# A recommender tower on one core: layers 2 and 3 turned round, the last two tables looked up whole, weights loaded later

## The reference

```
e = stack([tbl_0[ids[:, 0]], ..., tbl_25[ids[:, 25]]], axis=1)          # 512 x 26 x 128
all_emb = concatenate([bottom[:, None, :], e], axis=1)                  # 512 x 27 x 128
z = einsum('bfd,bgd->bfg', all_emb, all_emb)[:, TRIU_I, TRIU_J]         # 351 pairs
h = concatenate([z, bottom], axis=1)                                    # 479
h = maximum(h @ W_top1 + b_top1, 0)                                     # 512
h = maximum(h @ W_top2 + b_top2, 0)                                     # 256
y = h @ W_top3                                                          # 512 x 1
```

## Time and profile before

| | us |
|---|---|
| median of 3 runs | 107.83 (107.79 to 108.54) |
| the profiled execution, its own time | 108.94 |
| its span, first to last instruction | 107.2 |
| PE busy in the span | 99.5 (93%) |
| DVE, ACT, POOL busy | 65.0, 55.8, 59.8 |
| mean granted TensorE clock | 1.00 of 2.4 GHz |

### The profile page before, as it was taken

The page is one execution under the profiler, slowest core; times in us unless marked ns, Lnnn a source line. Parts: engine busy times, 40 slices in busy tenths (PEclk is TensorE's granted clock), DMA queues, the critical chain, the costliest instruction groups (busy, mean ns, idle before and its releaser), DMA issues.

```text
span 107.2 us, 3613 instructions
## 1 busy us (share of the span) xinstructions
PE 99.5 (93%) x1546; PEld 84.7 (79%) x1546; DVE 65.0 (61%) x146; ACT 55.8 (52%) x96; POOL 59.8 (56%) x65
## 2 busy tenths in 40 slices
PE   4999699999999999999878999979999989999992
PEld 4766476888888888888767999769898979997970
DVE  5597799999999999999970019005600740092000
ACT  5531959926976994993704324322462427224331
POOL 2777777777877777788777777777730000000000
DMA  2799898748768648995122121221210000000000
GB/s 47 221 337 329 271 282 295 230 68 320 215 135 317 165 137 229 299 269 132 49 55 55 49 55 49 69 64 51 55 54 2 6 6 0 6 6 0 0 0 3
DMA packets 7460, 13.22 MB, mean 123 GB/s; under 512 B 1990, under 2 KB 3881, under 8 KB 7444
## 3 DMA queue, kind: packets, MB, share of 16 engines
q1 hardware_dynamic: 5484, 9.25, 28.1%
q0 software_dynamic: 1792, 3.67, 13.1%
q10 hardware_dynamic: 168, 0.07, 0.3%
HBM read 12.97 MB, written 0.01 MB: 121 GB/s over the span
## 4 chain that ended last, share of the span: by engine, by line
PE 44%; DVE 36%; issue 8%; DMA 6%; ACT 2%; SPq 1%; ACTq 0%
DVE onehot L522 25%; PE acc L709 11%; PE acc L675 11%; DVE lo L505 10%; PE ring L719 7%; DMA raw<-tbl 6%; PE acc L640 6%; PE acc L700 4%; PE ring L652 3%; PE ring L729 2%; PE ring L683 1%; ACT hi L363 1%; DVE raw L493 1%; DVE idt L486 0%; ACT h L467 0%
## 5 line engine op out<-in xcount | busy, mean ns | idle before, releaser
L346 POOL DMA_INDIRECT rows<-tbl,ids_sb x56 | 59.0, 1054 | 18.3 <-issue 16.8
L522 DVE TENSOR_SCALAR onehot<-far 128x512 fp32r<-128x512 f32 x83 | 31.6, 437 | 1.3 <-ACT far L377 1.3
L613 PE MATMUL acc<-onehot,hi 128*128 128x512 f32 x84 | 24.3, 412 | 1.1 <-ACT hi L363 0.7
L613 PE MATMUL acc<-onehot,lo 128*128 128x512 f32 x84 | 22.7, 393 | 0.0
L532 DVE COPY gram<-acc 128x432 f32<-128x432 f32 x4 | 3.7, 921 | 28.5 <-PE acc L675 28.5
L613 PEld LDWEIGHTS acc<-onehot,hi 128*128 128x128 f32 x84 | 15.4, 194 | 5.5 <-DVE onehot L522 1.1
L363 ACT CAST hi<-raw 128x1024 fp32r<-128x1024 f32 (+1 forms) x11 | 12.0, 1087 | 12.9 <-issue 8.0
L613 PEld LDWEIGHTS acc<-onehot,lo 128*128 128x128 f32 x84 | 15.8, 188 | 3.6
L505 DVE TENSOR_TENSOR lo<-raw,hi 128x512 fp32r<-128x512 f32 (+1 forms) x24 | 16.8, 701 | 1.3 <-ACT hi L363 1.3
L675 PE MATMUL acc<-emb 128*27 128x27 f32 x1024 | 12.8, 192 | 1.6 <-issue 1.6
L675 PEld LDWEIGHTS acc<-emb 128*27 128x27 f32 x1024 | 10.8, 104 | 4.1 <-issue 2.7
(11 more groups left out here) (44 smaller groups left out, 82.8 us busy)
## 6 DMA issues: line engine op xcount, KB each, us to landing
raw<-tbl SPq DMA_DIRECT2D x9, 448.0 KB
raw<-tbl SPq DMA_DIRECT2D x2, 576.0 KB
ids_b<-ids SPq DMA_DIRECT2D x4, 256.0 KB, 4.5
rows<-tbl,ids_sb POOLq DMA_INDIRECT x56, 4.0
w1z<-w SPq DMA_DIRECT2D x1, 702.0 KB
raw<-tbl SPq DMA_DIRECT2D x10, 52.0 KB
w_sb<-w SPq DMA_DIRECT2D x1, 512.0 KB
raw<-tbl SPq DMA_DIRECT2D x1, 256.0 KB, 3.1
```

The source lines that it names most:

```text
L346: nc.gpsimd.indirect_dma_start(out=rows[:, t, slot, :], out_offset=None, in_=tables[table], in_offset=bass.IndirectOffsetOnAxis(ap=ids_sb[ ...
L522: ins = nc.vector.tensor_scalar(onehot[:, n % OH_RING, k, :], far[:, t % FAR_RING, :], row, None, ALU.is_equal)
L613: mm = nc.tensor.matmul(acc[:, look_bank(t), :], part_of[0:rows_of, t % HL_RING, c * D:(c + 1) * D], onehot[0:rows_of, n % OH_RING, k, :], ...
```

## The change

Five edits.

1. Tables 10 and 11 are looked up by `look`, 512 columns at once, like the others; `part` goes. ACT copies their sums in two pieces, tile 0 and tiles 1 to 3 (`emb_last`).
2. The order behind the lookups is new: the four `gram` steps of a tile stand together, and so do the four of `l1`. `turn` (2,0) moves ahead of the last lookup.
3. Layer 2 is turned round: `h1` is stationary and the weights move, 256 columns, so samples lie on the partitions. DVE adds the bias (L537 of the changed kernel), then takes relu, multiplies by a broadcast W_top3 and sums along the row in one instruction (L539). Layer 3 (`out`, L677) is one product that turns the column of 128 sums into a row.
4. All weights are issued when PE is through with table 9 (a wait of SP on `oh_used`). W_top3 and b_top2 are loaded broadcast to 128 partitions, 128 KB each, instead of 1 KB each.
5. The main part of table 1 is issued at the start from ACT's queue, and no longer by SP behind table 0.

```diff
-    for j in range(NL - 2):
-        order += [("compare", j + 1, 0), ("look", j, 0)]
+    for j in range(NL):
+        if j + 1 < NL:
+            order.append(("compare", j + 1, 0))
+        order.append(("look", j, 0))
...
+    order += [("bottom", 0, 0), ("bottom", 0, 1), *gram(0), ("turn", 2, 1), ("bottom", 1, 0), *gram(1), ("turn", 2, 2),
+              ("pairs", 0, 0), *l1(0), ("turn", 2, 3), ("bottom", 1, 1), ("pairs", 1, 0), *gram(2),
+              ("bottom", 2, 0), *l1(1), ("bottom", 2, 1), ("l2", 0, 0), ("turn", 3, 0), ("l2", 1, 0), ("bottom", 3, 0),
+              ("pairs", 2, 0), ("turn", 3, 1), *l1(2), ("out", 0, 0), ("bottom", 3, 1), ("turn", 3, 2), ("turn", 3, 3),
+              *gram(3), ("out", 1, 0), ("l2", 2, 0), ("pairs", 3, 0), *l1(3), ("out", 2, 0), ("l2", 3, 0), ("out", 3, 0)]
...
@@ SP
-            load_rows(1)
+            load_rest(1, raw_in[1])
...
+            sp.wait_ge(oh_used, 2 * (NL - 2))
             sp.dma_start(w1b[:], w1[ZC * ZK:, :]).then_inc(w1b_in, 16)
...
-            sp.dma_start(w3_sb[:], w3).then_inc(w_in, 16)
+            sp.dma_start(w3_b[:], w3.broadcast_to([128, H2])).then_inc(w_in, 16)
@@ ACT
             act.dma_start(ids_sb[:], ids).then_inc(ids_in, 16)
+            n = chunks(1) - 1
+            act.dma_start(raw[:, 1, 0:n * D], tables[LOOKED_UP[1]][0:KP * n, :].rearrange("(p k) d -> p (k d)", k=n)
+                          ).then_inc(raw_in[1], 16)
...
+                        if t == NL - 1:
+                            for a, e in ((0, 1), (1, TILES)):
+                                nc.scalar.copy(emb[:, a:e, :, first:first + 2],
+                                               acc[:, b:b + 2, a * LANES:e * LANES].rearrange("d j (t p) -> d t p j", p=LANES)
+                                               ).then_inc(emb_last, 1)
@@ DVE
+                    nc.vector.tensor_tensor(h2[:, t % 2, :], ring[:, b, 0:H2], b2_b[:], ALU.add).then_inc(h2_ready, 1)
+                    dve.wait_ge(h2_ready, t + 1)
+                    nc.vector.scalar_tensor_tensor(h2w[:, t % 2, :], h2[:, t % 2, :], 0.0, w3_b[:], ALU.max, ALU.mult,
+                                                   accum_out=y_col[:, t:t + 1]).then_inc(y_summed, 1)
@@ PE
-                        mm = nc.tensor.matmul(ring[:, b, 0:LANES], w2_sb[:, k, part * 128:(part + 1) * 128],
-                                              h1[:, t % 2, k, :], start=(k == 0), stop=(k == M1 - 1))
+                        pe.wait_ge(h1_ready, M1 * t + k + 1)
+                        mm = nc.tensor.matmul(ring[:, b, 0:H2], h1[:, t % 2, k, :], w2_sb[:, k, :],
+                                              start=(k == 0), stop=(k == M1 - 1))
...
+                    pe.wait_ge(y_summed, t + 1)
+                    nc.tensor.matmul(ring[0:1, b, 0:LANES], y_col[:, t:t + 1], ident[:], start=True, stop=True
+                                     ).then_inc(y_turned, 1)
```

More of the change, by code:

```diff
@@ L50 @@
 H1, H2 = 512, 256
-M1, M2 = H1 // 128, H2 // 128
+M1 = H1 // 128
 UNIT = 16
@@ L104, in work_order, with gram @@
             order.append(("turn", *behind[j]))
[L107 to L116, removed]
[5 rows of a table removed]
+    def gram(t):
+        return [("gram", t, part) for part in range(STEPS)]
@@ new lines, in l1 @@
+    def l1(t):
+        return [("l1", t, part) for part in range(M1)]
+    order += [("bottom", 0, 0), ("bottom", 0, 1), *gram(0), ("turn", 2, 1), ("bottom", 1, 0), *gram(1), ("turn", 2, 2),
[3 more added lines that the diff above has]
+              *gram(3), ("out", 1, 0), ("l2", 2, 0), ("pairs", 3, 0), *l1(3), ("out", 2, 0), ("l2", 3, 0), ("out", 3, 0)]
@@ L122, in work_order @@
     return order
 ORDER = work_order()
-USES = [s for s in ORDER if s[0] in ("turn", "pairs", "l2", "l3")]
+USES = [s for s in ORDER if s[0] in ("turn", "pairs", "l2", "out")]
 def bank(step, i, part=0):
@@ L423, in _ @@
                                        bot[:].rearrange("d (t q u) -> d t q u", t=TILES, q=Q)).then_inc(emb_bot, 1)
-                elif step == "part":
-                    samples, half = divmod(part, 2)
-                    if (t, half) == (NL - 1, 1):
-                        first, b = slot_of(NL - 2), part_bank(NL - 2, samples)
-                        act.wait_ge(part_done, samples + 1)
-                        nc.scalar.copy(emb[:, samples * TILES // PARTS:(samples + 1) * TILES // PARTS, :, first:first + 2],
-                                       acc[:, b:b + 2, 0:PART].rearrange("d j (t p) -> d t p j", p=LANES)
-                                       ).then_inc(emb_part, 1)
                 elif step == "turn":
@@ L468, in _ @@
                                              ACT.Relu, bias=b1_sb[:, m:m + 1]).then_inc(h1_ready, 1)
-                elif step == "l2":
-                    if t >= 2:
-                        act.wait_ge(l3_done, t - 1)
-                    if t == TILES - 1 and part == 1:
-                        continue
-                    b = bank(step, t, part)
-                    act.wait_ge(l2_done, M2 * t + part + 1)
-                    nc.scalar.activation(h2[:, t % 2, part, :], ring[:, b, 0:LANES], ACT.Relu,
-                                         bias=b2_sb[:, part:part + 1]).then_inc(h2_act, 1)
-                elif step == "l3":
+                elif step == "out":
                     b = bank(step, t)
-                    act.wait_ge(l3_done, t + 1)
+                    act.wait_ge(y_turned, t + 1)
                     nc.scalar.copy(y[0:1, t * LANES:(t + 1) * LANES], ring[0:1, b, 0:LANES]).then_inc(y_ready, 1)
@@ L567, in wait_emptied @@
                     pe.wait_ge(zt_ready, i + 1)
-                elif was == "l2" and (i, g) == (TILES - 1, 1):
-                    pe.wait_ge(h2_dve, 1)
                 elif was == "l2":
-                    pe.wait_ge(h2_act, M2 * i + g + 1)
-                elif was == "l3":
+                    pe.wait_ge(h2_ready, i + 1)
+                elif was == "out":
                     pe.wait_ge(y_ready, i + 1)
@@ L582, in _ @@
             for step, t, part in ORDER:
-                b = bank(step, t, part) if step in ("turn", "pairs", "l2", "l3") else None
+                b = bank(step, t, part) if step in ("turn", "pairs", "l2", "out") else None
                 if step == "compare":
@@ L659, in _ @@
                             pe.wait_ge(emb_bot, 1)
-                        pe.wait_ge(emb_part, 1 if t < TILES // PARTS else 2)
+                        pe.wait_ge(emb_last, min(t + 1, 2))
                         pe.wait_ge(emb_turned, turn_count(t, TURNS - 1))
                     n = UNITS * t + unit
-                    if n == GPS - 1 and rest == 0:
-                        pe.wait_ge(emb_part, 2)
                     if n >= GPS and rest == 0:
```

87 lines of the change are left out of this document (24 added, 63 removed), and 5 rows, old and new, of the table behind.

## The result

The changed kernel is slower: 120.15 us (median of 4 runs, 118.57 to 121.11) against 108.19 (107.79 to 111.51) for the kernel before on the same chip, a ratio of 1.107 with the interval 1.092 to 1.122. The forecast was 103.8 in a range of 102.7 to 106.2. The profiled execution took 121.11 with a span of 119.4. Ratios here leave out executions over 1.5% above the fastest of their kernel; medians and ranges hold all of them.

A forecast was written before the change was run, and what follows sets the result against it. PE's stream and its gaps were taken to set the end, DVE counting at the start and just before 55 us. Terms summed to -4.05: 108.94 became 104.9, less 1.1 to the median, 103.8 us; range 102.7 to 106.2.

The forecast's parts named there:

- Whole grams: Behind the lookups: grams put together spare PE the switches between steps, 16 steps in 4 runs, -0.3 us.
- The start: Table 1's load, issued earlier from ACT's queue, ends DVE's wait for it: -1.2 us, bounds 0 and 1.34.
- Rival 1: At the start: table 1 lands as late as before because all queues share 16 engines; 105.0 us, chance 0.18.
- The lookups: Tables 10 and 11 looked up whole save PE 3.0 us; the wait for ACT's copy before the first gram goes, -0.3.
- Layer 2: Turned round, 8 passes of 256 columns at 0.225 us, 1.80 a tile; only switches of tiles 0 and 1 go, -0.6.
- rival 3: 256-column passes of the turned layer cost only the lookups' price (0.144 us): 102.2 us, chance 0.06.
- Layer 3: Two passes for four, 0.3 for 0.61 us, and tile 2's relu wait shortened: -1.45 over tiles 0 to 2.
- the tail: From ACT's last relus to the end: 3.45 us for 3.24, taken as +0.2, between -0.1 and +0.8.
- -2.05: PE's saving in the two turned layers, made of the terms -0.6 and -1.45 us.
- The gaps: PE's waits in the new order behind the lookups: 4.75 us walked against 0.83 + 0.43 before, so +3.5.
- The weights: Issued at about 49 us instead of 40, all there at 57, wanted from 57 on: nothing waits, 0.
- Rival 5: Clock falls to 1.2 GHz in gaps around pairs (3), tile 3's l1 and l2 take twice as long: 108.2 us, chance 0.03.

The follow-up runs named there:

- shifted copy: The changed kernel with 16 one-column float32 matmuls (32 passes, no use to the result) ahead of the first lookup; 121.25 us in one run.

## Why the prediction was wrong, step by step

**The step that failed** is "Whole grams spare such switches too, 16 steps in 4 runs: -0.3", and with it the walk that took every `gram` of 256 passes at the price of 64. That price holds for a pass whose instructions are there. I asked what data and which PSUM bank each step waits for, and never whether PE's own instructions arrive. Against the walked span of 107.2 - 4.05 = 103.15 the profile has 119.4, so 16.25 more: 8.8 are the five waits; 5.5 the clock that falls behind them; about 1.5 more are small pauses within the runs of 209 and 128 passes (3.37 and 1.78, where the price of the earlier trace rows gives 2.3 and 1.4). The gaps that I did walk came out 1.1 smaller. The remaining 1.5 I did not trace. So the term of -0.3 came out as 8.8 + 5.5 = 14.3 of loss.

A sign stood in the rows. The earlier trace rows has "0.83 issue" at 69.53, and in PE's timeline of the kernel before it divides one `gram` step into 29 and 35 passes: a wait in the middle of a step, where no semaphore can be asked. I listed it among the old stream's gaps, as something that the new order would drop. In three profiles of the kernel before it is 0.83, 0.79 and 0.47, always before the same 35 passes. A wait of unnamed cause in the middle of a uniform run is a supply that is nearly exhausted.

**The start (-1.2)** came as described in the profile, and is still worth nothing: it was read from one execution in which table 1 was late. In both others of this kernel and in five profiles of other kernels with the same start it was ready at 7.6 to 7.9, and edits 4 and 5 together measure what edit 4 measures alone (0.998 and 0.997). I had the hint: that execution was 1.1 above the median, and I both credited the change with its lateness and subtracted the 1.1. Rival 1 (the start gives nothing) was right in its result. It was wrong in its reason: the table does not land late both times, it is on time both times. The Trainium skill (DMA: Bandwidth & Descriptors, "Issuing engines are not separate DMA queues") puts a second issuing engine's gain at the sequencer's time alone; by that the step was to be worth next to nothing. With the late weights the runs agree; alone it measured 1.010.

**The lookups (-3.0 and -0.3)** went as forecast: no wait for one-hots, the last of them through at 57.0, `bottom` at 57.01. But no version with whole lookups is faster than the kernel before, even where the grams are spread (ratios 0.999 to 1.013 in three, 109.62 against 109.32 in a fourth). In the fourth, which differs from the version with edits 4 and 5 in the whole lookups and the order that goes with them, the waits inside grams sum to 0.17 + 1.36 + 1.45 + 1.01 = 4.0, against 1.2 there. So what the 256-column lookups cost seems to have been partly time in which instructions arrived; no run parts this from the rest of the order.

**Layer 2** was priced rightly: eight passes from 88.73 to 90.46, 0.216 each for the 0.225 taken. Both bounds (0.272 and 0.144) and rival 3 are out. The formula that I quoted from the Trainium skill (TensorE: Matmul & The Clock Gate, "Back-to-back issue gap") is given there for a single isolated matmul, not for a stream; its 0.109 for 256 columns is half of the 0.216 here. **Layer 3** and the tail: DVE's new pair takes 0.42 and 0.43 (and 0.08 to read the accumulator) for the 0.49 and 0.45 taken; from the last relus (113.96) to ACT's copy (117.61) it is 3.65 against 3.24 before, so +0.4 for +0.2. The -2.05 that I gave to layers 2 and 3 is not borne out. With edit 4 they measure as 0.991, edit 4 alone as 0.997, on different chips and with intervals that overlap; beside edit 5 they are 1.006 and 1.010. In the two profiles set side by side above they save 0.06 up to the last `l1` and lose 0.3 in the tail. Part of what PE saves among spread grams turns into waits for instructions (0.50 and 0.23 there, 0.40 with edit 4 alone).

**The gaps (4.75 walked)** measured 0.57 before `l1` (0), 0.15 and 0.19 before `l2` (1) and `l1` (2), 0.80 before `gram` (3), 1.36 before `pairs` (3), 0.62 before `l1` (3): 3.7. This was the part I trusted least, and it came out close.

**The weights (0)** made no one wait. But their move does something that I had called nothing ("what they leave free at 40 us, no lookup was waiting for"): the gathers of 38 to 50 us land in 2.7 instead of 3.4 to 7.2, and the wait of 1.7 for rows goes. In the median it is not told from nothing (0.997, 0.991 to 1.003). The wait for rows was absent from the one profile that I had read, and so was any sign that a gather could be a gap.

**Rival 5** (the clock falls, 0.03) did happen, for a reason it didn't name: not the gaps around `pairs` (3), which without fetch waits left the clock at 1.00, but idle time of PE inside the grams. The Trainium skill (TensorE: Matmul & The Clock Gate, "HAM oscillation") warns of a stream in which work alternates with waits, longer ones than any here; in this trace the clock fell all the same, to 0.68 in the window from 70 us. The pieces at the lower clock cost 5.5. That this is near the 4.4 of the rival is chance: 4.4 was `l1` and `l2` of tile 3, and of these only `l1` (3) was slow, 1.6 us.

## What to carry to other kernels

Short matmuls spend instructions faster than long ones spend time, so ask of each dense run how many instructions it needs and how fast they come; here the blocks came every 3.7 us while PE used one up in 1.8 to 2.4. A wait marked "issue" in the middle of a uniform run is the sign. In such a place, taking wide, slow passes out from among the short ones may save nothing: four versions here that did so gained nothing. And read the gap that a term rests on in a second profiled execution before you credit the change with it: one execution's late DMA is not the kernel's.

## What the runs showed of the hardware

- The waits inside runs of short matmuls lie 128 passes (256 instructions), or a multiple of it, apart, and the queue of instructions moves one 16 KB packet for about as many (7 for 962 passes, 11 for 1474). Waits one block apart end 3.78 and 3.73 us apart in the changed kernel, 3.4 to 4.0 in its shifted copy and in the kernel with whole grams alone. The waits inside grams last 0.2 to 2.5 us, at places that move pass by pass with the stream; at the same place of the kernel before one took 0.83, 0.79 and 0.47.
- After idle times of 0.82, 1.42 and 1.95 us between 61 and 70 us the granted clock fell to 0.68 of full over the next ten, and 24 passes of 128 columns took 4.58 instead of 2.94. In the shifted copy 1.22, 0.83 and 1.50 at the same steps left it at 1.00 (24 passes in 2.94); it fell with waits of 1.70 and 2.45 behind them (4.78).
- The gathers issued between 38 and 50 us landed in 2.7 to 3.1 us (median of a profile) with the late weights and in 3.4 to 7.3 with the early ones; the kernel before had 3.4, 7.2 and 4.8 in three executions.
- A float32 pass of 256 columns costs 0.216 us, twice one of 128.
- What stays open: why a run of 209 passes is slow already before its wait (3.37 for some 2.3), and how an order could be built that keeps the whole lookups and feeds the grams; four tries here did not.
